# Both norms of a prelude as one factor, router and residual moved beside the feed-forward, value tiles copied by ScalarE

## The chip, the cores and the metric

The kernel runs on one NeuronCore of a Trainium2 chip, as one program in one launch. The metric is the device time of a run in microseconds. In the profile the engines are called PE (TensorE), DVE (VectorE), ACT (ScalarE), POOL (GpSimd) and SP (SyncE, which issues the transfers); PEld is TensorE's weight load.

## What is computed

Four layers, each a cross-attention followed by a feed-forward, on x of 4 x 256 tokens by 256 features (1024 tokens in eight tiles of 128) in float32. Ahead of every block stands a LayerNorm without weights, and x grows by the block's result. The change touches what stands ahead of the feed-forwards of layers 0 and 2. Their input x below is the LayerNorm's output, xn in the kernel:

```python
# layer 0
routed = sigmoid(x @ w_router + b_router) > 0.5
v = rmsnorm(x, norm1_w) @ wv + bv
h = x + v @ wo
h2 = rmsnorm(h, norm2_w)
mlp = (silu(h2 @ w_gate) * (h2 @ w_up)) @ w_down      # 704 wide
out = where(routed, h + mlp, x)

# layer 2: an attention of the tokens among themselves, then experts
h = rms(x, w_ln1)
q, k, v = h @ wq + bq, h @ wk + bk, h @ wv + bv       # 16 heads of 16
q, k = rope(q), rope(k)
scores = where(causal, q @ k.T * 16 ** -0.5, min)
x = x + softmax(scores) @ v @ wo
h = rms(x, w_ln2)                                     # router, 8 experts, a shared one
```

## The kernel before

The program is written by hand, one function for each engine and stage (`dve_pre0` is what VectorE does ahead of the feed-forward of layer 0). Each engine runs its own list in order and waits on semaphores; nothing is scheduled for it. The stages follow each other: latent attention 0, `pre0`, feed-forward 0, folded attention 1, `pre1`, feed-forward 1, folded attention 2, `pre2`, feed-forward 2, latent attention 3, `pre3`, feed-forward 3.

**Norms.** VectorE collects statistics of each tile of x as it is finished (line 245) and aggregates them (L257). The power -1/2 is taken by GpSimd on 8 columns (one for each token tile): `pool_ln` (L273) for the LayerNorm's factor rstd, `pool_pow` (L1747) for the RMS norm's rms_r. VectorE makes xn from x, mean and rstd (L268, eight tiles of 128x256), takes the RMS value out of the variance in three small steps (`dve_norm_ms`, L1759 to L1761), waits for the second power and writes z = xn * rms_r (L1769 in layer 0, L2231 in layer 2).

**pre0.** TensorE folds wv and wo into one matrix and turns bv into a bias row, runs filler matmuls (`pe_warm`, L287, that write to a free bank and are read by nobody), transposes z (L280), and for each tile multiplies by the fold (L1722) and adds the bias by a matmul with the identity (L1724). VectorE scores the router from xn (L1772), adds xn to x (L1776), and then, for each tile, adds the product to xn (L1782), adds it to x where the token is routed (L1785), and sums the squares (L1787). GpSimd takes the power, VectorE writes z2, TensorE transposes it, ScalarE and VectorE split it into a high and a low half-precision part (L1625, L1632), and the feed-forward begins with its first up matmul (L1401).

**Feed-forward.** `dve_ffn` and its sisters run over steps `st`, one for each half of a 128-wide column of hidden features: gate and up products (L1401 to L1403), activation (L1513), products (L1556, L1560), and, `LAG` = 8 steps later, the high part (ACT L1526), the low part (DVE `low`, L1575) and the down product (L1446 to L1448). Feed-forward 0 has 11 steps, so the loop goes on to step 17, and from step 11 on there is only the tail of downs. At its end x takes the sum of each tile out of PSUM (L1594).

**pre2.** GpSimd clears four areas for the value tiles (L2104) after its powers. TensorE transposes z, ScalarE scales it into xT (L2207), and for each of eight tiles TensorE computes q, k (L1961) and v (L1963). VectorE adds the bias to v (L1992) and to q and k (L1993), applies the rotation (L2010, L2012, L2017) and splits the transposed q and k (L1999, L2002); ScalarE makes the high parts (L1979, L1981); GpSimd copies v by head into the cleared areas (L2110). The self-attention runs over 32 steps of four heads' scores (L2032), with the causal mask added by a matmul at each step's end (L2035).

Of the kernel before, what the change touches and what calls it, by code (L numbers as in the profile page):

```python
# [91 lines left out]
def build(nc, d, out):  # L92
    ctx = ExitStack()
    with ctx:
# [98 lines left out]
        def bank(n, k=1):  # L193
# [1373 lines left out]
        def dve_ffn(n, begun=0):  # L1567
# [10 lines left out]
            for st in range(f.steps + LAG - 1):  # L1578
# [11 lines left out]
                if st >= LAG - 1:  # L1590
                    low(st - LAG + 1)
            for i in range(NT):
                dve.wait_ge(s.y_ps, NT // 2 * n + i // 2 + 1)
                dve.scalar_tensor_tensor(x[:, i, :], PS[:, 4 + i // 2, (i % 2) * D:(i % 2 + 1) * D],  # L1594
                                         UNDOWN if n else p0_route[:, i:i + 1], x[:, i, :], ALU.mult, ALU.add).then_inc(ffn_x, 1)
# [99 lines left out]
        p0_score, p0_route, p0_ssq = ffn_v[:, 528:536], ffn_v[:, 536:544], ffn_v[:, 544:552]  # L1695
        p0_junk = ffn_v[:, 1024:1280]
        z = shape3(ffn_s, NT, D)
# [6 lines left out]
        def pe_pre0():  # L1704
# [44 lines left out]
        def pool_pre0():  # L1749
            x_ready(nc.gpsimd, 1)  # L1750
            pool_ln(1)
            pool_pow(pre[0].ms, 1, rms_r[:], rms_e[:], pre[0].r)
# [3 lines left out]
        def dve_norm_ms(me, ready, r_done):  # L1756

            dve = nc.vector
            me.link(dve, dve.tensor_tensor(rms_e[:], rstd[:], rstd[:], ALU.mult))  # L1759
            me.link(dve, dve.tensor_tensor(rms_e[:], rms_e[:], meanvar[:, :, 1], ALU.mult))  # L1760
            dve.tensor_scalar(rms_e[:], rms_e[:], RMS_EPS, None, ALU.add).then_inc(ready, 1)  # L1761
            dve.wait_ge(r_done, 1)

        def dve_pre0():
            dve, s, me = nc.vector, pre[0], own["dve"]
            dve_ln(1)
            dve_norm_ms(me, s.ms, s.r)
            for i in range(NT):
                dve.tensor_scalar(z[:, i, :], xn[:, i, :], rms_r[:, i:i + 1], None, ALU.mult).then_inc(s.z, 1)  # L1769
            dve.wait_ge(s.w, 32)  # L1770
            for i in range(NT):
# [731 lines left out]
```

## Time and profile before

| | us |
|---|---|
| median of three runs | 1309.33 (1308.08 to 1310.52) |
| the profiled execution, its own time | 1310.3 |
| its span (first to last instruction) | 1308.5 |
| PE busy | 1217.0 (93%) |
| DVE busy | 878.1 (67%) |
| ACT busy | 505.6 (39%) |
| POOL busy | 372.8 (28%) |

Times in rows are microseconds from the start of the span. The granted clock of TensorE is a share of its full 2.4 GHz, and 0.979 is its mean over the span. Busy shares are means over all stages.

### The profile page before, as it was taken

How to read it: one execution, taken by the hardware profiler on the slowest of the kernel's cores; microseconds unless marked ns; L12 is line 12 of the kernel's file. 1: busy time of each engine (PE TensorE's matmuls, PEld its weight loads, DVE VectorE, ACT ScalarE, POOL GpSimd, SP SyncE). 2: the span in 40 equal slices, each digit the busy share in tenths (PEclk: the TensorE clock that was granted, in tenths of full speed). 3: DMA queues.
4: the chain of work that ended last, by engine and by line, in shares of the span. 5: the costliest groups of instructions: out<-in, count | busy, mean ns of one | idle time of the engine just before them, and what ended most of it. 6: DMA issues, size and time to landing. Idle time of an engine off the chain costs nothing.

```text
span 1308.5 us, 21984 instructions
## 1 busy us (share of the span) xinstructions
PE 1217.0 (93%) x8541; PEld 790.2 (60%) x8541; DVE 878.1 (67%) x1717; ACT 505.6 (39%) x1133; POOL 372.8 (28%) x385
## 2 busy tenths in 40 slices
PE   6889999999799999999999879998999898999997
PEld 4664658999546565665657545664556565456655
DVE  3776776677376666667667596777766757766666
ACT  3422460111133433433443225652443343555553
POOL 1510115565203333334113320000333333133332
PEclk9899999999899999999999997999999979999999
DMA  4030141000144444444410000000443200233342
GB/s 143 2 153 17 51 141 37 1 1 1 46 174 113 123 124 121 113 113 122 151 58 1 17 1 1 2 2 15 128 122 123 96 17 2 86 115 113 114 133 82
DMA packets 41544, 97.20 MB, mean 74 GB/s; under 512 B 5446, under 2 KB 18246, under 8 KB 39392
## 3 DMA queue, kind: packets, MB, share of 16 engines
q1 hardware_dynamic: 41440, 95.79, 23.8%
q8 instruction: 68, 1.11, 0.4%
q14 instruction: 36, 0.29, 0.1%
HBM read 94.35 MB, written 1.42 MB: 73 GB/s over the span
## 4 chain that ended last, share of the span: by engine, by line
PE 78%; DVE 13%; ACT 3%; issue 3%; POOL 2%; DMA 1%; SPq 0%; DVEq 0%; POOLq 0%; ACTq 0%
PE PS L1401 10%; PE PS L1402 10%; PE PS L1403 10%; PE PS L1446 5%; PE PS L1448 4%; PE PS L1447 4%; PE PS L1036 3%; PE PS L1054 2%; PE PS L1220 2%; PE PS L2050 2%; PE PS L2067 2%; PE PS L1022 2%; PE PS L1024 2%; PE PS L1023 2%; PE PS L2032 1%
## 5 line engine op out<-in xcount | busy, mean ns | idle before, releaser
L1616 POOL TENSOR_TENSOR arena<-arena,m_g 128x512 f32<-128x512 f32 x142 | 183.1, 1291 | 409.9 <-DMA m_g<-gate_rows 240.3
L1401 PE MATMUL PS<-arena 128*128 128x512 f16 x608 | 230.8, 380 | 4.7 <-DVE arena L1632 1.8
L1402 PE MATMUL PS<-arena 128*128 128x512 f16 x608 | 230.8, 380 | 0.0
L1403 PE MATMUL PS<-arena 128*128 128x512 f16 x608 | 230.7, 379 | 0.0
L1446 PE MATMUL PS<-arena 128*128 128x256 f16 x608 | 165.9, 273 | 9.5 <-DVE arena L1573 8.7
L1448 PE MATMUL PS<-arena 128*128 128x256 f16 x608 | 165.7, 273 | 0.0
L1447 PE MATMUL PS<-arena 128*128 128x256 f16 x608 | 165.7, 273 | 0.0
L1513 ACT ACTIVATE arena<-PS 128x512 f32<-128x512 f32 x112 | 66.9, 597 | 245.9 <-PE PS L1403 235.5
L1556 DVE SCALAR_TENSOR_TENSOR arena<-arena,PS 128x512 f32<-128x512 f32 x112 | 77.0, 688 | 124.1 <-ACT arena L1513 123.9
L1573 DVE TENSOR_TENSOR arena<-arena 128x512 f16<-128x512 f32 x142 | 112.0, 789 | 3.9 <-ACT arena L1523 3.9
L1403 PEld LDWEIGHTS PS<-arena 128*128 128x128 f16 x608 | 59.5, 98 | 71.9 <-issue 0.3
L1401 PEld LDWEIGHTS PS<-arena 128*128 128x128 f16 x608 | 59.5, 98 | 65.4 <-DVE arena L1560 2.9
L1523 ACT ACTIVATE arena<-arena 128x512 f16<-128x512 f32 x142 | 88.0, 620 | 22.2 <-PE PS L1448 17.7
L1402 PEld LDWEIGHTS PS<-arena 128*128 128x128 f16 x608 | 59.5, 98 | 58.2 <-issue 0.3
L1102 POOL TENSOR_TENSOR arena<-arena 128x256 f32<-128x256 f32 x96 | 67.6, 726 | 79.3 <-DVE arena L1130 79.3
L1560 DVE TENSOR_TENSOR arena<-arena,PS 128x512 f32<-128x512 f32 x112 | 77.1, 688 | 15.0 <-PE PS L1403 1.0
L1446 PEld LDWEIGHTS PS<-arena 128*128 128x128 f16 x608 | 59.4, 98 | 37.6 <-issue 12.7
L1447 PEld LDWEIGHTS PS<-arena 128*128 128x128 f16 x608 | 59.4, 98 | 19.0
L1448 PEld LDWEIGHTS PS<-arena 128*128 128x128 f16 x608 | 59.4, 98 | 7.0
L2127 ACT ACTIVATE arena<-PS,arena 128x128 f32<-128x128 f32 (+1 forms) x128 | 52.0, 420 | 26.2 <-DVE arena L2141 25.7
L1480 DVE SCALAR_TENSOR_TENSOR arena<-w_stage,arena 128x512 f16<-128x512 f32 x80 | 57.0, 714 | 6.7 <-ACT arena L1475 6.7
L1553 DVE TENSOR_TENSOR arena<-arena,PS 128x512 f32<-128x512 f32 x44 | 30.2, 686 | 45.1 <-PE PS L1403 45.1
(282 smaller groups left out, 2301.2 us busy)
## 6 DMA issues: line engine op xcount, KB each, us to landing
w_stage<-in_up SPq DMA_DIRECT2D x80, 256.0 KB, 2.9
m_g<-gate_rows SPq DMA_DIRECT2D x70, 256.0 KB, 4.2
arena<-in_heads SPq DMA_DIRECT2D x16, 1088.0 KB, 6.5
w_stage<-in_down SPq DMA_DIRECT2D x80, 128.0 KB, 4.1
m_g<-gate_rows SPq DMA_DIRECT2D x17, 512.0 KB, 4.0
m_g<-gate_rows SPq DMA_DIRECT2D x6, 448.0 KB, 4.6
m_g<-gate_rows SPq DMA_DIRECT2D x6, 384.0 KB, 4.1
m_g<-gate_rows SPq DMA_DIRECT2D x6, 320.0 KB, 4.0
```

The source lines that it names most:

```text
L1102: ins = pool.tensor_tensor(r[:, f, :], r[:, f, :], p2[:, 1 - f, :], ALU.add)
L1401: pe.matmul(to, w_hi, x_hi, start=(k == 0), stop=False)
L1402: pe.matmul(to, w_lo, x_hi, start=False, stop=False)
L1403: ins = pe.matmul(to, w_hi, x_lo, start=False, stop=(k == KT - 1))
L1446: pe.matmul(to, h_hi, w_hi, start=(c == 0 and i % 2 == 0), stop=False)
L1447: pe.matmul(to, h_hi, w_lo, start=False, stop=False)
L1448: ins = pe.matmul(to, h_lo, w_hi, start=False, stop=False)
L1523: act.activation(hid_part(0, st % 2), m_c[:, st % 2, :], ACT.Copy).then_inc(s.hi, 1)
L1556: dve.scalar_tensor_tensor(a, t, 1.0, g_ps, ALU.add, ALU.mult).then_inc(s.a, 1)
L1560: dve.tensor_tensor(m_b[:, st % LAG, :], a, u_ps, ALU.mult).then_inc(s.prod, 1)
L1573: dve.tensor_tensor(hid_part(1, st % 2), m_c[:, st % 2, :], hid_part(0, st % 2), ALU.subtract).then_inc(s.lo, 1)
L1616: pool.tensor_tensor(m_c[:, st % 2, :], m_b[:, st % LAG, :], m_g[:, st // 2 % 2, st % 2, :], ALU.mult).then_inc(s.c, 1)
```

## The change

1. **Norms.** `dve_both_norms` takes the place of `dve_ln` and `dve_norm_ms` in `pre0` and `pre2`. The variance of xn is var / (var + 1e-5), so both factors together are (var + 1e-6 (var + 1e-5)) to the power -1/2, and z is written from x directly. GpSimd takes this power first and rstd after it. xn is made later: in `pre0` behind z, in `pre2` one tile at a time inside the self-attention.
2. **pre0.** The bias matmul goes. GpSimd adds the bias row to each xn tile and writes it to p0_h; VectorE adds the product from PSUM to p0_h and sums the squares of the tile before.
3. **Router and residual** of layer 0 go into the feed-forward's loop (`dve_routed`): steps 0 to 7 score a tile each, step 8 makes the masks, steps 8 to 15 write x for a tile each with two instructions.
4. **Filler matmuls**: 30 become 13 ahead of z2 in `pre0`, 41 become 16 ahead of z in `pre2`.
5. **Value tiles.** ScalarE copies v out of PSUM without bias, and GpSimd adds the bias where it copied.
6. **Mask.** In score steps with 128 keys the mask matmuls come first and open the sum; with 256 keys they stay last.

```diff
 # dve_ffn
+                if n == 0:
+                    dve_routed(own["dve"], st)
...
 # pe_pre0
                 for k in range(KT):
-                    pe.matmul(PS[:, 4 + i // 2, (i % 2) * D:(i % 2 + 1) * D], zT[:, k, i, :], p0_fold[:, k, :],
-                              start=(k == 0), stop=False)
-                ins = pe.matmul(PS[:, 4 + i // 2, (i % 2) * D:(i % 2 + 1) * D], ident[:], p0_bias, start=False, stop=True)
+                    ins = pe.matmul(PS[:, 4 + i // 2, (i % 2) * D:(i % 2 + 1) * D], zT[:, k, i, :], p0_fold[:, k, :],
+                                    start=(k == 0), stop=(k == KT - 1))
...
-            pe_warm(30, 3)
+            pe_warm(13, 3)
...
 # pool_pre0
+            pool_pow(s.ms, 1, rms_r[:], rms_e[:], s.r)
             pool_ln(1)
-            pool_pow(pre[0].ms, 1, rms_r[:], rms_e[:], pre[0].r)
+            pool.wait_ge(s.fold, 2)
+            for i in range(NT):
+                pool.wait_ge(ln.xn, NT + i + 1)
+                pool.tensor_tensor(p0_h[:, i, :], xn[:, i, :], p0_bias, ALU.add).then_inc(s.biased, 1)
...
+        def dve_both_norms(me, m, s):
+            dve = nc.vector
+            for i in range(NT):
+                ins = dve.bn_aggr(meanvar[:, i, :], stats[:, i, :])
+            me.link(dve, ins)
+            dve.tensor_scalar(var_e[:], meanvar[:, :, 1], LN_EPS, None, ALU.add).then_inc(ln.var, 1)
+            dve.wait_ge(ln.var, m + 1)
+            dve.scalar_tensor_tensor(rms_e[:], var_e[:], RMS_EPS, meanvar[:, :, 1], ALU.mult, ALU.add).then_inc(s.ms, 1)
+            dve.wait_ge(s.r, 1)
+            for i in range(NT):
+                dve.tensor_scalar(z[:, i, :], x[:, i, :], meanvar[:, i, 0:1], rms_r[:, i:i + 1],
+                                  ALU.subtract, ALU.mult).then_inc(s.z, 1)
...
 # dve_qkv, biased(i)
-                dve.tensor_tensor(sa_v[:, i, :], PS[:, 2 + i % 2, 0:D], p2_bias[:, 2 * D:3 * D], ALU.add)
...
 # act_qkv
+            def copied(i):
+                act.wait_ge(s.qkv, i + 1)
+                act.activation(sa_v[:, i, :], PS[:, 2 + i % 2, 0:D], ACT.Copy).then_inc(s.copied, 1)
...
+            for i in range(NT):
+                copied(i)
+                if i:
+                    high(i - 1)
+            high(NT - 1)
...
 # pool_values
-                pool.wait_ge(s.biased, i + 1)
+                pool.wait_ge(s.copied, i + 1)
...
-                    ins = pool.tensor_copy(sa_vm[b][:, k, :, a, a, :], source[:, :, a, :])
+                    ins = pool.tensor_tensor(sa_vm[b][:, k, :, a, a, :], source[:, :, a, :], bias[:, :, a, :], ALU.add)
...
 # dve_self
+                if t % SA_OF_Q == 1:
+                    dve_normed(5, t // SA_OF_Q)
...
 # pe_pre2
-            pe_warm(41, 2)
+            pe_warm(16, 2)
```

How VectorE's list in `pre0` stands before, from the aggregation to the first turn of the per-tile loop (xn and x are the token tiles, rms_e and rms_r the input and output of the power, arena holds z, masks and constants):

```order
L257 BN_AGGR meanvar<-stats 128x2 x8
L259 TENSOR_SCALAR var_e<-meanvar 128x8
L268 TENSOR_SCALAR xn<-x,meanvar,rstd 128x256 x8
L1759 TENSOR_TENSOR rms_e<-rstd 128x8
L1760 TENSOR_TENSOR rms_e<-rms_e,meanvar 128x8
L1761 TENSOR_SCALAR rms_e<-rms_e 128x8
L1769 TENSOR_SCALAR arena<-xn,rms_r 128x256 x8
L1772 SCALAR_TENSOR_TENSOR arena<-xn,arena 128x256 x8
L1776 TENSOR_TENSOR x<-x,xn 128x2048
L1782 TENSOR_TENSOR xn<-xn,PS 128x256
L1785 SCALAR_TENSOR_TENSOR x<-PS,arena,x 128x256
L1787 SCALAR_TENSOR_TENSOR arena<-xn 128x256
```

And now:

```order
L1769 BN_AGGR meanvar<-stats 128x2 x8
L1771 TENSOR_SCALAR var_e<-meanvar 128x8
L1773 SCALAR_TENSOR_TENSOR rms_e<-var_e,meanvar 128x8
L1776 TENSOR_SCALAR arena<-x,meanvar,rms_r 128x256 x8
L1781 TENSOR_SCALAR xn<-x,meanvar,rstd 128x256 x8
L1790 TENSOR_SCALAR arena<-arena 128x2
L1803 TENSOR_TENSOR arena<-arena,PS 128x256 x2
L1796 SCALAR_TENSOR_TENSOR arena<-arena 128x256
L1803 TENSOR_TENSOR arena<-arena,PS 128x256
```

z (L1776) stands ahead of xn (L1781) and behind one power, the router's products and the long add are gone, and a turn of the loop is L1803 and L1796.

GpSimd's list at the same place, where L1750 and L1747 are the same helper's power and L1760 the bias add:

```order
+L1750 TENSOR_TENSOR rms_r<-rms_e,half_neg 128x8
 L273 TENSOR_TENSOR rstd<-var_e,half_neg 128x8
-L1747 TENSOR_TENSOR rms_r<-rms_e,half_neg 128x8 x2
+L1760 TENSOR_TENSOR arena<-xn,arena 128x256 x8
+L1750 TENSOR_TENSOR rms_r<-rms_e,half_neg 128x8
```

The power for z moved ahead of the one for rstd, and eight adds came in between that and the power for z2.

VectorE's list in steps 10 to 13 of feed-forward 0 now (L1575 is `low`, L1493 a low part of a down weight, L1827 and L1828 write x):

```order
L1575 SCALAR_TENSOR_TENSOR arena<-arena 128x512
L1827 SCALAR_TENSOR_TENSOR x<-xn,arena,x 128x256
L1828 SCALAR_TENSOR_TENSOR x<-arena,x 128x256
L1493 SCALAR_TENSOR_TENSOR arena<-w_stage,arena 128x256
L1575 SCALAR_TENSOR_TENSOR arena<-arena 128x512
L1827 SCALAR_TENSOR_TENSOR x<-xn,arena,x 128x256
L1828 SCALAR_TENSOR_TENSOR x<-arena,x 128x256
L1575 SCALAR_TENSOR_TENSOR arena<-arena 128x512
```

Before, this stretch held the L1575 and L1493 rows alone.

## Rows read from the trace of the kernel before

**Rows 1.** Windows: length, busy (count) of PE, PEld, DVE, ACT, POOL; granted clock, DMA

```profile
77.14:110.88 33.74, 29.14 (x140) 20.76 (x141) 27.48 (x98) 7.01 (x18) 4.92 (x3) 0.95 0.37 149
747.11:785.91 38.80, 30.68 (x118) 16.77 (x119) 35.76 (x74) 9.79 (x26) 9.89 (x16) 1.00 0.05 14
...
86.74:90.15 3.41, 3.41 (x14) 3.03 (x14) 3.20 (x16) 2.71 (x8) 0.00 (x0) 0.50 0.99 409
789.88:803.53 13.65, 13.65 (x76) 6.76 (x70) 6.92 (x10) 6.77 (x34) 0.00 (x0) 0.50 0.00 1
```

**Rows 2.** Timeline, norms of layer 0: start, duration, engine, line, operation, count, [idle before]

```profile
78.60 1.65 POOL L273 TENSOR_TENSOR rstd<-var_e,half_neg 128x8 f32<-128x8 f32 x1 [6.94 <-DVE var_e L259]
...
79.86 2.97 PE L287 MATMUL PS<-causal_b,ident_b 128*128 128x512 bf16 x13
...
80.28 2.67 DVE L268 TENSOR_SCALAR xn<-x,meanvar,rstd 128x256 f32<-128x256 f32 x8 [1.83 <-POOL rstd L273]
...
85.19 2.19 DVE L1769 TENSOR_SCALAR arena<-xn,rms_r 128x256 f32<-128x256 f32 x8 [1.75 <-POOL rms_r L1747]
...
85.60 2.97 PE L280 MATMUL PS<-ident,arena 128*128 128x128 f32 x16 [2.77 <-DVE arena L1769]
```

**Rows 3.** Timeline, the per-tile loop of layer 0 and what follows

```profile
95.74 0.42 DVE L1787 SCALAR_TENSOR_TENSOR arena<-xn 128x256 f32<-128x256 f32 x1
...
96.20 0.42 DVE L1782 TENSOR_TENSOR xn<-xn,PS 128x256 f32<-128x256 f32 x1
...
98.32 1.03 PE L1722 MATMUL PS<-arena 128*128 128x256 f32 x4
...
99.18 0.59 PE L1724 MATMUL PS<-arena,ident 128*128 128x256 f32 x2
...
99.61 6.64 PE L287 MATMUL PS<-causal_b,ident_b 128*128 128x512 bf16 x30
...
103.35 0.17 DVE L1789 TENSOR_SCALAR rms_e<-arena 128x8 f32<-128x8 f32 x1
...
110.88 0.39 PE L1401 MATMUL PS<-arena 128*128 128x512 f16 x1 [1.80 <-DVE arena L1632]
```

**Rows 4.** Single lines over the whole span: duration ns min/median/max, first and last start

```profile
L2104 POOL MEMSET arena<- x4: 951/977/978, 739.9 to 743.0; 128x1024 f32 x4
...
L2231 DVE TENSOR_SCALAR arena<-xn,rms_r x8: 334/674/1114, 740.0 to 744.8; 128x256 f32<-128x256 f32 x8
...
L1102 POOL TENSOR_TENSOR arena<-arena x96: 716/726/736, 202.9 to 332.6; 128x256 f32<-128x256 f32 x96
```

**Rows 5.** Timeline, norms of layer 2, one engine at a time

```profile
731.34 9.01 PE L287 MATMUL PS<-causal_b,ident_b 128*128 128x512 bf16 x41
...
733.45 1.64 POOL L273 TENSOR_TENSOR rstd<-var_e,half_neg 128x8 f32<-128x8 f32 x1 [7.12 <-DVE var_e L259]
...
740.03 5.16 DVE L2231 TENSOR_SCALAR arena<-xn,rms_r 128x256 f32<-128x256 f32 x8 [1.75 <-POOL rms_r L1747]
...
747.11 1.95 PE L1961 MATMUL PS<-arena,xT 128*128 128x512 f32 x4 [1.44 <-ACT xT L2207]
```

**Rows 6.** Timeline in feed-forward 1, GpSimd and VectorE

```profile
500.94 1.27 POOL L1616 TENSOR_TENSOR arena<-arena,m_g 128x512 f32<-128x512 f32 x1 [4.24 <-DMA m_g<-gate_rows]
...
501.81 0.95 DVE L1480 SCALAR_TENSOR_TENSOR arena<-w_stage,arena 128x512 f16<-128x512 f32 x1
```

**Rows 7.** Timeline, one tile of the QKV stretch of layer 2, VectorE

```profile
757.58 0.41 DVE L1992 TENSOR_TENSOR arena<-PS,arena 128x256 f32<-128x256 f32 x1
757.91 0.68 DVE L1993 TENSOR_TENSOR arena<-PS,arena 128x512 f32<-128x512 f32 x1
...
761.93 0.41 DVE L1992 TENSOR_TENSOR arena<-PS,arena 128x256 f32<-128x256 f32 x1
```

**Rows 8.** Timeline, the end of feed-forward 0, VectorE

```profile
151.85 0.69 DVE L1575 SCALAR_TENSOR_TENSOR arena<-arena 128x512 f16<-128x512 f32 x1 [0.74 <-ACT arena L1526]
...
153.42 0.69 DVE L1575 SCALAR_TENSOR_TENSOR arena<-arena 128x512 f16<-128x512 f32 x1 [0.55 <-ACT arena L1526]
```

More of the change, by code:

```diff
@@ L1770, in dve_pre0 @@
             dve.wait_ge(s.w, 32)
-            for i in range(NT):
-                me.link(dve, dve.scalar_tensor_tensor(p0_junk, xn[:, i, :], 1.0, p0_router, ALU.mult, ALU.mult,
-                                                      accum_out=p0_score[:, i:i + 1]))
-            me.link(dve, dve.tensor_scalar(p0_route, p0_score, p0_b, 0.0, ALU.add, ALU.is_gt))
             me.link(dve, dve.tensor_scalar(p0_n2s, p0_n2, SPLIT, None, ALU.mult))
-            me.link(dve, dve.tensor_tensor(x[:], x[:], xn[:], ALU.add))
@@ L1971, in pe_qkv @@
             pe.wait_ge(s.biased, NT)
+            pe.wait_ge(s.copied, NT)
             pe.wait_ge(s.qT, NT)
@@ L1975, in act_qkv, with high @@
             act, s = nc.scalar, pre[2]
-            for i in range(NT):
+            def copied(i):
+                act.wait_ge(s.qkv, i + 1)
+                act.activation(sa_v[:, i, :], PS[:, 2 + i % 2, 0:D], ACT.Copy).then_inc(s.copied, 1)
+            def high(i):
                 b, q = divmod(i, QT)
@@ L2027, in pe_scores, with mask @@
             both = [PS[:, n, 0:2 * keys].rearrange("p (a c) -> p a c", a=2) for n in range(8)[score_banks(t)]]
+            def mask(begins):
+                for e in range(2):
+                    ins = pe.matmul(both[e][:, :, keys - P:keys], ident_b[:], mask_self.rearrange("p (a c) -> p a c", a=2),
+                                    start=begins, stop=not begins)
+                return ins
+            if q == 0:
+                mask(True)
             for q_part, k_part in ((0, 0), (0, 1), (1, 0)):
@@ L2031, in pe_scores @@
                     rows = slice(32 * (j % 4), 32 * (j % 4) + 32)
-                    pe.matmul(both[e], sa_qT[rows, b, q, q_part, j // 4, :], sa_kT[rows, b, k_part, j // 4, :, 0:keys],
-                              start=(q_part == 0 and k_part == 0), stop=False)
-            for e in range(2):
-                ins = pe.matmul(both[e][:, :, keys - P:keys], ident_b[:], mask_self.rearrange("p (a c) -> p a c", a=2),
-                                start=False, stop=True)
-            ins.then_inc(s.s, 1)
+                    ins = pe.matmul(both[e], sa_qT[rows, b, q, q_part, j // 4, :], sa_kT[rows, b, k_part, j // 4, :, 0:keys],
+                                    start=(q == 1 and q_part == 0 and k_part == 0), stop=(q == 0 and q_part == 1))
+            (ins if q == 0 else mask(False)).then_inc(s.s, 1)
         def pe_self():
@@ L2227, in dve_pre2 @@
             dve, s, me = nc.vector, pre[2], own["dve"]
-            dve_ln(5)
-            dve_norm_ms(me, s.ms, s.r)
-            for i in range(NT):
-                dve.tensor_scalar(z[:, i, :], xn[:, i, :], rms_r[:, i:i + 1], None, ALU.mult).then_inc(s.z, 1)
+            dve_both_norms(me, 5, s)
             dve.wait_ge(s.w, 48)
```

65 lines of the change are left out of this document (41 added, 24 removed).

## The prediction

> **What bounds the kernel now.** I read the busy shares by stretch first, then the timeline of the two preludes that the diff touches, with the row's releaser for who ends each wait. The kernel is one long chain of stages with no slack between them, so microseconds saved in a stage are saved at the end, provided that they lie on that stage's own chain. What lies there differs by stage. In the prelude of the first feed-forward (77.14 to 110.88 us) nothing runs through: VectorE waits for GpSimd's power, 1.65 us a time, TensorE waits for VectorE's normalised tiles, and after that VectorE's own queue sets the pace [rows 1, 3]. TensorE needs 1.29 us for a tile of the folded product and is done at 99.8, but VectorE's per-tile loop ends at 103.35 [rows 3]. In the QKV stretch of layer 2 VectorE is busy 35.76 of 38.80 us, TensorE 30.68 [rows 1]: VectorE is the bound there. Elsewhere TensorE is, busy for 93% of the span, except in the last steps of a feed-forward, where a value goes round from ScalarE to VectorE to TensorE [rows 8].
>
> **The change, part by part.**
>
> *Norm of layer 0.* Before: one power (78.60), eight normalised tiles in 2.67 us (80.28), three small steps of about 0.2 us, a second power, eight tiles z from 85.19 [rows 2]. After: one small step more, one power (78.8 to 80.45), then z straight from x, eight at 0.33 us. TensorE cannot take them before 82.83, when its 13 filler matmuls end [rows 2]. That is 2.8 us earlier than the 85.60 of before. The second power, now for rstd, runs on GpSimd behind the first while VectorE writes z. Here is the first unknown, the SBUF port. The trace has two cases of it. A tile like z takes 0.334 us alone, and 1.114 us when one of GpSimd's four memsets (0.977 us) is ahead of it: the tile ends just after the memset, four times in a row [rows 4]. And a two-input VectorE instruction issued at 501.81 under a GpSimd add that ends at 502.21 takes 0.95 us and not 0.69 [rows 6, 8]. So I take it that GpSimd's instruction holds VectorE up to its end, for the power too, which no row shows: z then ends at 84.5 instead of 83.1.
>
> *Adds on GpSimd beside VectorE's tiles.* xn now comes behind z, and each xn tile feeds a GpSimd add 128x256 of 0.73 us [rows 4]. Two xn tiles get through before the first add, the other six wait for one add each, at 0.73 + 0.09 us (the memset and tile pair take 1.03 for a memset of 0.95 to 0.98) [rows 4]. xn therefore ends near 90.1, not at 87.2, and a small step on VectorE waits for one more add: the loop starts at 91.0.
>
> *The per-tile loop.* VectorE drops one instruction of three, and the router's eight products and the 2048-column add ahead of it. What is left is one PSUM add (0.34, as 757.58 to 757.91) and one square (0.46, 95.74 to 96.20) [rows 3, 7]: 0.80 a tile, 8 x 0.80 + 0.46 = 6.9, and 0.3 for the first square behind the last GpSimd add: 98.1. TensorE gives its last tile at 84.95 + 8 x 0.86 = 91.8 (0.86 is 98.32 to 99.18, the bias matmul being gone) [rows 3], earlier, so it isn't the bound. 98.1 against 103.35 is 5.3 us gained, and 7.53 us from there to the first up matmul stay [rows 3]. Without any port hold TensorE would set the pace: loop end 93.9, gain 9.4.
>
> *Filler matmuls.* 13 instead of 30 end at 91.8 + 13 x 0.22 = 94.7 [rows 3], z2 comes at 100.3: 5.6 us without work on TensorE. Before, 2.8 us without work (82.83 to 85.60) were followed by 3.41 us at a granted 0.50, which is 1.2 GHz [rows 1, 2]. I expect that again, partly in the 16 transposes of z2 and perhaps in the first up matmuls: 1.5 us lost, 0 to 3.
>
> *Router and residual in the feed-forward.* Steps 0 to 7 get one product (0.46), steps 8 to 15 two (0.92). While ups run, VectorE's gaps and TensorE's extra down work take them. From step 11 on there are only downs; VectorE's idle time there is 0.74 and 0.55 us a step [rows 8], mean 0.65, against 0.92 added, in five steps: 5 x 0.27 = 1.3 us lost. Bounds: 0, if TensorE's matmuls are the slower link, and 3.
>
> Layer 0 together: -5.3 + 1.5 + 1.3 = -2.5 us.
>
> *Norm of layer 2.* The power starts at 733.65 and ends at 735.3; z began at 740.03 [rows 5]. The rstd power now stands ahead of the four memsets. With everything held, z0 waits for the power, z1 to z4 for a memset each: last z at 735.3 + 1.65 + 4 x 1.03 + 3 x 0.26 + 0.3 = 742.2, where it was 745.2. The QKV product starts 3.0 us earlier than 747.11. If the power holds nothing, six z tiles are through before the first memset, the last ends at 739.1, and the gain is 6.1. Filler 16 instead of 41 ends at 731.34 + 16 x 0.22 = 734.9 [rows 5], so TensorE has little to do until 742; a stretch at half clock costs me 0.8 (0 to 2.6), since QKV waits for VectorE anyway.
>
> *Value tiles.* VectorE loses 757.58 to 757.91, 0.33 us in each of eight tiles of 4.35 us [rows 7]: -2.7 us. ScalarE is busy 9.79 us in the stretch, so its copy has room, and TensorE's work (30.68 less 21 filler matmuls of 0.22, over eight tiles: 3.25 us) stays below the 4.02 that VectorE then needs. GpSimd now adds two inputs instead of copying. It is released by ScalarE, about when VectorE's last two-input instruction of the tile runs, and its adds then lie beside PSUM instructions. Cost 0; if they fall on two-input instructions, up to the whole 2.7.
>
> *Mask ahead, xn in the self-attention.* The same eight matmuls per step behind the same wait: 0. Eight xn tiles (0.33 each) go into VectorE's gaps: 0.3, at most 2.6. The spell at half clock from 789.88, 13.65 us [rows 1], follows a wait that stays, so I leave it.
>
> Layer 2 together: -3.0 + 0.8 - 2.7 + 0.3 = -4.6. Sum -7.1 us: 1310.3 of the profiled execution become 1303.2; the median of the three runs, 1309.3, is 1.0 lower, so 1302.
>
> **The port by the skill.** The Trainium skill, "SBUF — State Buffer", section "Who interferes with whom", says that the port pair of VectorE and GpSimd is an exclusive lock, taken for a whole instruction by whoever issues first. By that rule the rstd power holds z as the memset did, which is the forecast; were the lock shorter than the instruction, the first rival below would come out.
>
> **The rivals.**
> - *The power does not hold the port* (its operands are 8 columns), adds and memsets do. Layer 0 gains 1.4 more, layer 2 3.1 more: 1297.5. For it: 1.64 us for 8 columns can hardly be port traffic. Against: nothing shown.
> - *No hold by the adds either*, clock unharmed: -9.4 + 1.3 - 6.1 - 2.7 + 1 = -16, 1293.5. Against it is the 0.95 us of [rows 6].
> - *Part of the gain is given back*: the adds in QKV hold VectorE's two-input instructions by 0.33 us a tile (+2.7), and half clock reaches 3.4 us into the first ups (+1.7): 1306.4. For it: GpSimd's copy is released just ahead of these instructions today, so a small shift brings the adds there.
> - *Slower*: with the filler before layer 2 cut, TensorE stays at half clock through QKV. A tile would take 2 x 3.25 = 6.5 us instead of 4.02, so 8 x 2.5 = 20 us lost against 7.1 gained: 1322. It decides from the third tile on, 7.1 / 2.5 = 2.8. Against it: after idle time the clock came back within 3.41 us when TensorE was busy [rows 1]; for it: the other spell, 13.65 us under busy rows.
> - *The edits gain nothing* because other work sets the stage: excluded in the norms, where VectorE and TensorE both sit idle for the power.
>
> **How the numbers follow.** Forecast 0.45, the power free of the port 0.25, no hold 0.08, part given back 0.17, slower 0.05. About 0.2% (2.6 us) is what a measurement can tell here. Faster by more than that, below 1306.7: the first three and over half of the fourth, 0.87. Same 0.08, slower 0.05. Forecast's own range 1299.5 to 1305; with the neighbours, for eight in ten, 1295.5 to 1306.5.
>
> **What the profile after would show.** z tiles of layer 0: if the first is near 1.7 us long the power holds, if 0.4 it doesn't. xn tiles at about 0.8 us pace beside the adds, or at 0.33. The last square of the loop near 98 us on the span's clock, not 103; QKV tiles 4.0 us apart; the down steps at the end of the first feed-forward 1.7 to 1.8 us apart instead of 1.5. I am wrong if a half-clock stretch lies in QKV, if the z2 power starts later than 99, or if the self-attention stretch grows by over 1 us.

## The result and the profile after

The changed kernel took 1296.11 us (median of 4 runs, 1295.07 to 1297.61). The kernel before took 1309.33 us, the median of three runs; a fourth took 2074.97 us and is left out. These times make a ratio of 0.9899 and 13.2 us. The ratio on record for this set is 0.9874 (95% interval 0.9851 to 0.9897); it does not come out of the times listed with it, and the record does not say why. Two later sets of rounds with the same two kernels gave 0.9899 (0.9877 to 0.9921) and 0.9905 (0.9890 to 0.9920). So the change takes 12 to 13 us off by the times, up to 17 by the first ratio, where 7 were forecast. The profiled execution took 1295.07 us, its span is 1293.2.

I cut both traces at the same instructions (first fold product, first up of each feed-forward, first x of its end, first aggregation of layer 2's statistics, first QKV product, first score, the squares' sum behind the self-attention):

| stretch | before, us | after, us | change | forecast |
|---|---|---|---|---|
| prelude of layer 0, to the first up | 33.72 | 26.57 | -7.15 | -3.8 |
| feed-forward 0, to its first x | 44.23 | 46.16 | +1.93 | +1.3 |
| norm of layer 2, to the first QKV product | 14.65 | 9.21 | -5.45 | -3.0 |
| QKV product, to the first score | 38.79 | 37.10 | -1.70 | -1.9 |
| self-attention | 103.80 | 98.75 | -5.05 | +0.3 |
| all other stretches | 1073.33 | 1075.37 | +2.04 | 0 |

The forecast -1.9 is -2.7 for the value tiles and +0.8 for half clock. The norms and the self-attention are where it missed. One warning on the cuts: with the mask ahead, the first two mask matmuls (0.31 us) lie before the first score, so they count in the QKV stretch and not in the self-attention. Where kernels with the mask first and last are compared below, I cut at the first matmul of the self-attention, mask or score. No run makes the norms' edit, or the prelude's, alone: what each part is worth within the -7.15 and the -5.45 us is read from the timelines.

The timeline of layer 0 after, which answers [rows 2, 3]:

```profile
78.48 1.65 POOL L1750 TENSOR_TENSOR rms_r<-rms_e,half_neg 128x8 f32<-128x8 f32 x1 [7.95 <-DVE rms_e L1773]
80.11 1.81 POOL L273 TENSOR_TENSOR rstd<-var_e,half_neg 128x8 f32<-128x8 f32 x1
80.17 2.67 DVE L1776 TENSOR_SCALAR arena<-x,meanvar,rms_r 128x256 f32<-128x256 f32 x8 [1.83 <-POOL rms_r L1750]
...
82.77 5.98 DVE L1781 TENSOR_SCALAR xn<-x,meanvar,rstd 128x256 f32<-128x256 f32 x8
83.31 6.70 POOL L1760 TENSOR_TENSOR arena<-xn,arena 128x256 f32<-128x256 f32 x8 [1.39 <-DVE xn L1781]
...
86.33 7.07 PE L1726 MATMUL PS<-arena 128*128 128x256 f32 x32
89.38 0.75 DVE L1803 TENSOR_TENSOR arena<-arena,PS 128x256 f32<-128x256 f32 x2
...
95.78 0.17 DVE L1809 TENSOR_SCALAR rms_e<-arena 128x8 f32<-128x8 f32 x1
...
98.11 3.46 PE L280 MATMUL PS<-ident,arena 128*128 128x128 f32 x16 [1.91 <-DVE arena L1812]
...
103.42 0.39 PE L1401 MATMUL PS<-arena 128*128 128x512 f16 x1 [0.55 <-DVE arena L1634]
```

The reader is to see one pair first: z (L1776) runs from 80.17 under the rstd power of 80.11 and keeps 2.67 us for eight tiles, 0.33 each; six of the eight begin before that power ends at 81.92. The power does not hold VectorE. xn (L1781), the same operation, runs under the adds and takes 5.98. In layer 2, which answers [rows 5], z starts with the same power above it and then meets the memsets:

```profile
729.65 1.82 POOL L273 TENSOR_TENSOR rstd<-var_e,half_neg 128x8 f32<-128x8 f32 x1
729.72 4.82 DVE L1776 TENSOR_SCALAR arena<-x,meanvar,rms_r 128x256 f32<-128x256 f32 x8 [1.82 <-POOL rms_r L1750]
...
731.23 4.21 POOL L2157 MEMSET arena<- 128x1024 f32 x4
...
736.06 1.36 PE L1996 MATMUL PS<-arena,xT 128*128 128x512 f32 x2 [1.02 <-ACT xT L2263]
```

The windows after (length, busy of PE, PEld, DVE, ACT, POOL, granted clock, DMA share, GB/s), which answer [rows 1]; the last four are at half clock:

```profile
77.00:103.42 26.42, 23.96 (x107) 17.56 (x108) 22.33 (x69) 7.25 (x18) 11.78 (x11) 0.85 0.47 189
736.06:773.15 37.09, 32.45 (x119) 17.68 (x119) 32.06 (x66) 12.85 (x34) 7.47 (x16) 0.95 0.05 15
...
74.57:81.40 6.83, 6.32 (x15) 4.52 (x16) 3.23 (x17) 0.00 (x0) 2.92 (x2) 0.50 0.51 186
98.47:101.88 3.41, 3.41 (x17) 3.05 (x17) 3.38 (x11) 2.78 (x7) 0.00 (x0) 0.50 0.00 0
736.76:740.17 3.41, 3.41 (x6) 1.69 (x5) 1.00 (x2) 0.19 (x1) 0.00 (x0) 0.50 0.47 154
777.72:781.13 3.41, 3.41 (x23) 2.02 (x22) 2.00 (x4) 2.27 (x13) 0.00 (x0) 0.50 0.00 0
```

The first of the four, a spell, as I call such a stretch at half clock, lies over the fold product and was not there in the kernel before. It doesn't explain the gain: the changed kernel's two other profiles (after_again and after_third, below) ran the fold product at full clock, and there the stretch to the first up took 26.73 us, not 26.57.

The spell in the self-attention, 13.65 us in the kernel before [rows 1], is 3.41 us here. Is that the change's doing?

One QKV tile after, VectorE and GpSimd, which answers [rows 7]:

```profile
754.17 0.42 DVE L2045 TENSOR_TENSOR arena<-PS,arena 128x256 f16<-128x256 f32 x1
754.20 0.88 POOL L2163 TENSOR_TENSOR arena<-arena 128x128 f32<-128x128 f32 x2 [2.71 <-ACT arena L2015]
...
755.28 0.68 DVE L2039 TENSOR_TENSOR arena<-PS,arena 128x512 f32<-128x512 f32 x1
...
756.61 0.75 DVE L2058 TENSOR_TENSOR arena<-arena 128x256 f32<-128x256 f32 x2
...
759.12 0.68 DVE L2039 TENSOR_TENSOR arena<-PS,arena 128x512 f32<-128x512 f32 x1
```

From 755.28 to 759.12 a tile takes 3.84 us, against 4.35 [rows 7]. GpSimd's adds lie beside instructions that read PSUM, L2045 first, not beside the two-input L2058.

The end of feed-forward 0 after, which answers [rows 8]:

```profile
141.27 0.69 DVE L1575 SCALAR_TENSOR_TENSOR arena<-arena 128x512 f16<-128x512 f32 x1
141.87 0.48 DVE L1827 SCALAR_TENSOR_TENSOR x<-xn,arena,x 128x256 f32<-128x256 f32 x1
142.39 0.48 DVE L1828 SCALAR_TENSOR_TENSOR x<-arena,x 128x256 f32<-128x256 f32 x1
142.91 0.69 DVE L1575 SCALAR_TENSOR_TENSOR arena<-arena 128x512 f16<-128x512 f32 x1
```

No idle time is left: VectorE sets the pace, 1.64 us here and 1.98 where a weight's low part comes in.

### The profile page after: what moved, and what is told of

Its sections match the earlier page's. It is cut to its first block, busy times and chain, and to the rows that moved or that the text cites. A ratio compares the mean times of both kernels' runs of the same rounds, so it can differ in the third digit from the quotient of the medians.

```text
span 1293.2 us, 21914 instructions
## 1 busy us (share of the span) xinstructions
PE 1203.8 (93%) x8483; PEld 783.6 (61%) x8483; DVE 882.1 (68%) x1713; ACT 508.9 (39%) x1141; POOL 376.6 (29%) x393
## 3 DMA queue, kind: packets, MB, share of 16 engines
q1 hardware_dynamic: 41440, 95.79, 24.0%
## 4 chain that ended last, share of the span: by engine, by line
PE 76%; DVE 15%; issue 3%; ACT 3%; POOL 1%; DMA 1%; SPq 0%; DVEq 0%; POOLq 0%; ACTq 0%
PE PS L1401 10%; PE PS L1402 10%; PE PS L1403 10%; PE PS L1446 4%; PE PS L1448 4%; PE PS L1447 4%; PE PS L1036 3%; PE PS L1054 2%; PE PS L1220 2%; PE PS L2103 2%; PE PS L1022 2%; PE PS L1024 2%; PE PS L1023 2%; PE PS L2120 2%; DVE small L547 1%
## 5 line engine op out<-in xcount | busy, mean ns | idle before, releaser
L1480 DVE SCALAR_TENSOR_TENSOR arena<-w_stage,arena 128x512 f16<-128x512 f32 x80 | 62.9, 788 | 5.4 <-ACT arena L1475 5.4
```

## The experiments

Theory A: the gain is the removed power and VectorE's removed work; GpSimd's adds and memsets hold VectorE, powers don't, and the spell in the self-attention has nothing to do with the change. Theory B, the rival: the change itself shortened the spell, by the mask or the value tiles.

### One part alone, and one part undone: the mask and the value tiles

**mask_only** is the kernel before with this part of the diff alone:

```diff
+            if q == 0:
+                mask(True)
             for q_part, k_part in ((0, 0), (0, 1), (1, 0)):
...
+            (ins if q == 0 else mask(False)).then_inc(s.s, 1)
```

> The kernel before with the mask's two matmuls ahead of the scores (for steps of 128 keys) and nothing else of the change. By the prediction (the same eight matmuls behind the same wait) it is worth 0: 1309 us, self-attention stretch 103.8 us. Rival, from the trace after, where the period of four such steps went from 10.01 to 9.90 and 12.45 to 12.23 us: 0.1 us a step, 1.3 to 1.5 us over the stretch, so 1308 us. A second question rides on it: the spell at 1.2 GHz from 789.88 us, 13.65 us long in the kernel before and 3.41 us after. If it hangs on this edit, the spell is short here too and the stretch loses about 5 us (1304 us); if it hangs on what comes before the stretch or on where the window of the clock falls, it stays at 13.65 us.

**values_only** is the kernel before with ScalarE's copy of a value tile and GpSimd's add:

```diff
+                act.activation(sa_v[:, i, :], PS[:, 2 + i % 2, 0:D], ACT.Copy).then_inc(s.copied, 1)
...
-                dve.tensor_tensor(sa_v[:, i, :], PS[:, 2 + i % 2, 0:D], p2_bias[:, 2 * D:3 * D], ALU.add)
...
-                    ins = pool.tensor_copy(sa_vm[b][:, k, :, a, a, :], source[:, :, a, :])
+                    ins = pool.tensor_tensor(sa_vm[b][:, k, :, a, a, :], source[:, :, a, :], bias[:, :, a, :], ALU.add)
```

> The kernel before with the value tiles copied by ScalarE and the bias added by GpSimd, nothing else. By the prediction's sum the QKV product loses 0.33 us in each of eight tiles, 2.7 us: 1306.6 us. By the trace after, where VectorE's two-input instruction of 0.94 us also became 0.75 us since GpSimd no longer runs beside it, it is 0.51 us a tile, 4.1 us: QKV stretch (first product to first score) 38.8 to 34.7 us, 1305 us, provided that no half clock falls into its first tile. The spell at 1.2 GHz in the self-attention: stays at 13.65 us if the mask is its cause.

**mask_last** is the changed kernel with the mask behind the scores again:

> The changed kernel with the mask's matmuls back behind the scores. By the periods of the four-step groups the mask ahead is worth 0.1 us a step (9.90 against 10.01, 12.23 against 12.45), 1.3 to 1.5 us in all: self-attention 100.1 us with a short spell, 104 with a long one, the whole 1297.5 us. By the prediction it is worth 0.

mask_only: 0.9990 of before (0.9975 to 1.0006), which alone tells nothing. values_only: 0.9976 (0.9958 to 0.9995). The stretches say more. In both profiles 10.24 us at half clock lay over the start of the QKV product (from 745.36 and 744.73 us), so they compare with each other: it took 41.73 us in mask_only, 41.41 without the 0.31 us of mask matmuls that lie ahead of the first score there, and 37.95 in values_only. The value edit is worth 3.5 us there, not the 2.7 forecast. mask_last: 0.9908 (0.9893 to 0.9923), self-attention 104.04 us, with a long spell. The changed kernel with a long spell (after_again, below) took 102.72 from its first score and 103.03 from its first mask matmul. So the mask ahead is worth 1.0 us in this pair, and not the 1.3 that the first scores alone would say. Behind the spell the same eight score steps repeat every 22.45 us in mask_last and every 22.13 in after_again. The windows, first mask_last, its self-attention and its spell:

```profile
774.07:878.11 104.04, 100.58 (x902) 61.65 (x903) 77.80 (x128) 57.65 (x264) 0.00 (x0) 0.93 0.01 1
778.60:792.26 13.66, 13.54 (x71) 6.76 (x72) 6.92 (x12) 6.82 (x32) 0.00 (x0) 0.50 0.00 1
```

and the changed kernel again, after_again:

```profile
776.32:879.04 102.72, 98.82 (x901) 62.37 (x901) 77.55 (x129) 57.65 (x264) 0.00 (x0) 0.93 0.01 1
780.57:794.23 13.66, 13.55 (x72) 7.01 (x74) 6.99 (x11) 6.88 (x32) 0.00 (x0) 0.50 0.01 1
```

Where the gain of 0.1 us in a step comes from, TensorE of mask_last in a step of 128 keys (L2096 transposes, L2078 scores on 32 rows, L2081 the mask on 128 rows):

```profile
819.47 1.09 PE L2096 MATMUL PS<-ident,arena 128*128 128x128 f32 x8
820.50 0.50 PE L2078 MATMUL PS<-arena 32*128 32x256 f16 x6
```

and the same place in after_again (L2103 transposes, L2078 the mask):

```profile
821.04 1.09 PE L2103 MATMUL PS<-ident,arena 128*128 128x128 f32 x8
821.97 0.38 PE L2078 MATMUL PS<-causal_b,ident_b 128*128 128x256 bf16 x2
```

Eight transposes occupy 1.03 us when a 32-row matmul follows and 0.93 when a 128-row matmul does. The rows show the two prices and not their reason. "The same eight matmuls" have a price that depends on their order.

Neither edit alone gives the short spell: in mask_only it was 6.83 us, in values_only 17.07. But 6.83 is shorter than 13.65, so one profile each doesn't refute Theory B. What does is the same kernel once more.

### The spell: the same kernel again, and fillers

**after_again** and **after_third** are the changed kernel, unchanged.

> The changed kernel once more, unchanged, on the chip and in the rounds of the next ones. Time 1296 us. Its profile is one more look at the spell at 1.2 GHz at the head of the self-attention: in the profiles so far it is short (3.41 us) where it begins 4.38 us or more behind the first score, and 13.65 us where it begins 4.28 us or less behind it, whatever the edits ahead. If that holds, this profile is of one of the two kinds, and the self-attention takes 98.7 or 102.7 us by it. Rival: the spell's length hangs on the kernel, then it is 3.41 us again whatever the offset.

> The changed kernel, unchanged, in the rounds of the next one. Time 1296 to 1300 us; spell in the self-attention 13.65 us if it begins less than 4.3 us behind the first score, 3.41 us if it begins later.

1299.60 and 1299.79 us, the ratios given at the top. The profile of the first had the long spell, that of the second the short one, so the kernel's code does not decide it, and Theory B is gone. All profiles whose self-attention code is that of the changed kernel, sorted by the time from the first score to the spell's start:

| kernel | to the spell, us | spell, us | self-attention, us |
|---|---|---|---|
| pow_wide | 4.09 | 13.66 | 102.64 |
| bias_te | 4.12 | 13.65 | 102.64 |
| one_residual | 4.13 | 13.65 | 102.65 |
| memset_late | 4.19 | 13.65 | 102.67 |
| after_again | 4.25 | 13.66 | 102.72 |
| early_residual | 4.28 | 13.65 | 102.74 |
| more_filler | 4.38 | 3.42 | 98.74 |
| after_third | 4.45 | 3.42 | 98.75 |
| the changed kernel | 4.57 | 3.41 | 98.75 |
| adds_late | 4.73 | 3.41 | 98.76 |

The self-attention takes 4.0 us more when the spell is long. In all ten profiles it is long where it begins at 4.28 us or earlier and short from 4.38 us on; no run set that time on purpose, so this is an order found in the profiles and not a shown cause. With the mask last it was long at 4.53 too, so the border is not the same for other code.

**sa_filler** puts work where TensorE was idle:

```diff
-            pe_warm(8, 7)
+            pe_warm(11, 7)
...
             for t in range(SA_AHEAD):
                 pe_scores(t)
+            pe_warm(7, 3)
             for t in range(SA_STEPS):
                 turned(t)
```

> The changed kernel with 11 filler matmuls instead of 8 behind the QKV product and 7 more between the second step's scores and the first transposes, where TensorE is idle for 0.8 and 1.6 us. If TensorE's idle time there is what lowers the clock in the self-attention, no spell at 1.2 GHz follows within 20 us of the first score, and the self-attention takes 98 us in every execution, 1 to 4.5 us less than in the changed kernel: 1293 us. Rival: the waits of the first steps (for the maxima and exponentials) lower it anyway; then a spell of 3.4 or 13.7 us stays and the time is 1296 us or, if the fillers hold the transposes back, 1297 us.

0.9858 of before (0.9837 to 0.9879), beside 0.9899 for the changed kernel in the same rounds. Its self-attention, and a window from the QKV product to the end of it:

```profile
776.47:874.06 97.59, 94.50 (x908) 60.33 (x908) 77.23 (x128) 57.70 (x264) 0.00 (x0) 1.00 0.01 1
742.71:871.67 128.96, 121.88 (x1015) 75.65 (x1014) 105.81 (x182) 69.69 (x296) 7.47 (x16) 1.00 0.01 3
```

The granted clock is 1.00 over all of it. (The second window begins where an earlier spell ends, 6.83 us over the first QKV tiles.) all_three, below, has the same fillers and no spell from the QKV product to the end of the self-attention. The transposes after the fillers started 2.83 us behind the first score, exactly as early as without (779.30 against 776.47 here, 776.26 against 773.43 in early_residual), so the fillers cost nothing. So TensorE's idle time at the head of the self-attention brings the spell: filled, it is gone in both profiles, and the time is 1294.81 us beside 1299.60.

### What holds VectorE: memsets, adds, powers

**memset_late**, a wait ahead of the four memsets of layer 2:

```diff
+            pool.wait_ge(s.z, NT)
             for b in range(B):
                 me.link(pool, pool.memset(sa_vm[b], 0.0))
```

> The changed kernel with GpSimd's four memsets in layer 2 behind the eighth z tile, not beside the z tiles. If the memsets hold VectorE (z took 4.82 us for eight tiles there, beside 4.21 us of memsets, against 2.67 us in layer 0), z takes 2.7 us, the QKV product starts 2.1 us earlier against the last wait, and the kernel takes 1294 us. Rival: z is slow for a reason of its own (its operands, the statistics behind it): z stays at 4.8 us and the time at 1296 us. A loss is possible where the memsets now lie beside VectorE's router work: up to 4 us.

The z tiles and the memsets of memset_late:

```profile
728.50 2.67 DVE L1776 TENSOR_SCALAR arena<-x,meanvar,rms_r 128x256 f32<-128x256 f32 x8 [1.81 <-POOL rms_r L1750]
...
731.23 2.97 POOL L2158 MEMSET arena<- 128x1024 f32 x3 [0.98 <-DVE arena L1776]
731.28 0.93 DVE L1645 TENSOR_SCALAR arena<-arena 128x18 f16<-128x18 f32 x1
732.25 0.18 DVE L1646 SCALAR_TENSOR_TENSOR arena<-arena 128x18 f16<-128x18 f32 x1
...
733.42 0.69 DVE L1480 SCALAR_TENSOR_TENSOR arena<-w_stage,arena 128x512 f16<-128x512 f32 x1 [1.00 <-ACT arena L1475]
```

z takes 2.67 us instead of 4.82; the memsets hold. Even the small L1645, 0.18 us in the changed kernel, takes 0.93 under one. They don't hold everything: the SCALAR_TENSOR_TENSOR instructions behind it, L1646 and L1480, begin under the next memsets and take 0.18 and 0.69 us, as they do alone. The QKV product starts 1.8 us earlier (7.38 us behind the first aggregation, not 9.21), and the half-clock spell over its first tiles is gone, so it takes 35.39 us, not 37.10. Yet the median is 1296.10 us, a ratio of 0.9873 that no measurement here tells from the changed kernel's, since the earlier start met the long spell (4.19 in the table): 3.5 us won, 3.9 given back.

**adds_late**, GpSimd's bias adds of layer 0 behind the last xn tile:

```diff
             pool.wait_ge(s.fold, 2)
+            pool.wait_ge(ln.xn, 2 * NT)
             for i in range(NT):
```

> The changed kernel with GpSimd's eight bias adds in layer 0 behind the last xn tile, not beside the xn tiles. If the adds hold VectorE while they run (xn took 5.98 us for eight tiles beside 6.70 us of adds, z 2.67 us beside the power), xn takes 2.7 us here and the adds then run into the loop of PSUM adds and squares: its end moves from 95.31 to between 93 and 96 us on the span's clock, the whole by -2 to +1 us. Rival: xn waits for something else, then it stays at 6 us and the end comes 5 us later.

VectorE and GpSimd of adds_late:

```profile
83.02 2.67 DVE L1782 TENSOR_SCALAR xn<-x,meanvar,rstd 128x256 f32<-128x256 f32 x8
...
85.81 5.95 POOL L1761 TENSOR_TENSOR arena<-xn,arena 128x256 f32<-128x256 f32 x8 [3.64 <-DVE xn L1782]
...
86.56 7.07 PE L1726 MATMUL PS<-arena 128*128 128x256 f32 x32
88.55 0.75 DVE L1804 TENSOR_TENSOR arena<-arena,PS 128x256 f32<-128x256 f32 x2 [2.79 <-PE PS L1726]
...
95.79 0.17 DVE L1810 TENSOR_SCALAR rms_e<-arena 128x8 f32<-128x8 f32 x1
```

xn is through 3.06 us earlier on the span's clock, so the adds do hold it. But VectorE then idles 2.79 us for TensorE's first pair of tiles, and the loop ends at 95.79, where it was 95.78 (0.25 us better at most, since this execution's fold product began 0.26 us later). In this execution the hold was real and worth next to nothing: TensorE's product, whose last tile is done at about 93.6, closed in on it. But this profile has the spell over the fold product too (74.78 to 81.61), and it makes TensorE's product late: that starts 9.45 us behind the first fold product here and 9.48 in the changed kernel's first profile, but 7.25 in after_again, after_third and every other changed kernel whose fold ran at full clock. No profile has late adds and a fold at full clock, so there the hold can be worth up to about 2 us more (my estimate, 9.45 - 7.25). The time, 0.9881 of before (0.9843 to 0.9918), leaves that open.

**bias_te** takes the adds away and gives TensorE its bias matmul back:

```diff
+                ins = pe.matmul(PS[:, 4 + i // 2, (i % 2) * D:(i % 2 + 1) * D], ident[:], p0_bias, start=False, stop=True)
...
-                pool.tensor_tensor(p0_h[:, i, :], xn[:, i, :], p0_bias, ALU.add).then_inc(s.biased, 1)
...
-                dve.tensor_tensor(p0_h[:, i, :], p0_h[:, i, :], PS[:, 4 + i // 2, (i % 2) * D:(i % 2 + 1) * D], ALU.add).then_inc(me.sem, 1)
+                dve.tensor_tensor(p0_h[:, i, :], xn[:, i, :], PS[:, 4 + i // 2, (i % 2) * D:(i % 2 + 1) * D], ALU.add).then_inc(me.sem, 1)
```

> The changed kernel with the bias of the fold added by TensorE again (the matmul with the identity) and no add on GpSimd; the PSUM add reads xn. xn takes 2.7 us, since nothing runs beside it. TensorE's product takes 1.29 us a tile instead of 0.86, so it ends 3.4 us later than 92.4 and sets the loop's end: 96.6 us instead of 95.3, the whole 1.3 us slower than the changed kernel. If GpSimd's hold were the only thing that mattered, the end would be 92 us and the whole 3 us faster.

Ratio 0.9902 (0.9871 to 0.9933). Its stretch to the first up is 27.25 us, against 26.57 and against 26.00 in adds_late. xn took 2.67 us, and VectorE waited for TensorE's bias matmul at each of the four pairs:

```profile
87.86 0.75 DVE L1799 TENSOR_TENSOR arena<-xn,PS 128x256 f32<-128x256 f32 x2 [1.46 <-PE PS L1728]
...
90.45 0.42 DVE L1799 TENSOR_TENSOR arena<-xn,PS 128x256 f32<-128x256 f32 x1 [1.49 <-PE PS L1728]
...
93.04 0.42 DVE L1799 TENSOR_TENSOR arena<-xn,PS 128x256 f32<-128x256 f32 x1 [1.03 <-PE PS L1728]
```

**pow_wide** adds a power on 128x32 elements behind the one for z:

> The changed kernel with one more power on GpSimd, on 128x32 elements, right behind the power for z, so that all eight z tiles of layer 0 run beside it. In the changed kernel z ran at 0.33 us a tile beside a power on 128x8 elements (1.81 us). If a power never holds VectorE, z still takes 2.67 us; if it was the small size, z is held and ends with the power or is slower by a part. The whole is slower by the power's length less what hides it, 2 to 6 us, in both cases.

1302.98 us, one run. The power and the z tiles:

```profile
81.09 5.42 POOL L1757 TENSOR_TENSOR arena<-var_e,half_neg 128x32 f32<-128x32 f32 x1
81.16 2.67 DVE L1779 TENSOR_SCALAR arena<-x,meanvar,rms_r 128x256 f32<-128x256 f32 x8 [1.83 <-POOL rms_r L1750]
```

All eight tiles lie inside one instruction of GpSimd and none is held. The instruction's length is not what decides: a power of 5.42 us holds nothing, an add of 0.73 [rows 4] holds. What does decide stays open, since these powers had 8 or 32 columns and these adds 256: no run has a power on 256 columns or an add on 8.

### Fillers ahead of the norms

**more_filler** has `pe_warm(24, 3)` for 13 and `pe_warm(20, 2)` for 16.

> The changed kernel with 24 filler matmuls instead of 13 ahead of the z2 transposes and 20 instead of 16 ahead of layer 2's norm. If TensorE's idle time ahead of these places (1.91 us before the z2 transposes, then 3.41 us at 1.2 GHz from 98.47; the spell from 736.76 over the first QKV tile, which took 4.45 us and not 2.82) is what lowers the clock, one or both spells go: the z2 transposes take 2 us and not 3.46, the first QKV tile 2.8 us and not 4.45, 1 to 3 us together, 1294 us. Rival: the spells come for other reasons and stay, or the fillers themselves hold the transposes back: 1296 to 1297 us.

Ratio 0.9892 (0.9859 to 0.9924), no gain. The transposes of z2 ran at full clock, 2.28 us instead of 3.46, but the first up came only 0.3 us earlier against the fold (26.25 us, not 26.57): ScalarE and VectorE behind them set the pace. The spell over the first QKV tile stayed (736.83 to 740.24); memset_late, whose transposes no longer wait for held z tiles, lost it.

### The residual in the feed-forward

**early_residual** does two router products in each of steps 0 to 3 and the residual in steps 4 to 11; **one_residual** gives GpSimd two adds a tile and VectorE one product:

```diff
+            for i in range(NT):
+                pool.wait_ge(ffn.prod, FFNS[0].steps0 + i + 1)
+                pool.tensor_tensor(x[:, i, :], x[:, i, :], xn[:, i, :], ALU.add)
+                pool.tensor_tensor(p0_h[:, i, :], p0_h[:, i, :], xn[:, i, :], ALU.subtract).then_inc(s.biased, 1)
...
-                me.link(dve, dve.scalar_tensor_tensor(x[:, i, :], xn[:, i, :], p0_other[:, i:i + 1], x[:, i, :], ALU.mult, ALU.add))
```

> The changed kernel with the router's products two a step in steps 0 to 3 and the two residual products of a tile in steps 4 to 11 instead of 8 to 15. The prediction put 1.3 us on the steps that have only downs, the trace after shows 1.93 us for the feed-forward. If VectorE's two extra instructions are the slow link only where no ups run, the stretch from first up to first x goes from 46.16 to 44.6 us or less (44.23 before the change), the whole 1.5 us faster than the changed kernel. Rival: VectorE has no room beside the ups either: the steps 4 to 7 get longer by as much, 46.2 us.

> The changed kernel with h - xn and x + xn made by GpSimd in steps 0 to 7, so that VectorE has one instruction of 0.52 us a tile instead of two. If VectorE's time is the bound of the last steps, the feed-forward takes 44.6 us or less instead of 46.16; GpSimd's 16 adds of 0.73 us lie beside VectorE's instructions in steps 0 to 7 and may hold each by up to 0.73 us, which TensorE hides if it is the bound there. Rival: the hold is larger than TensorE's cover, then the first steps get longer by 1 to 6 us.

early_residual: 46.26 us for the stretch, the rival. The steps with only downs ran at 1.5 us again, but the first `low` came 23.53 us behind the first up, not 22.07. A step with ups leaves VectorE 0.77 or 0.17 us beside one product of the router in the changed kernel; beside two, in early_residual, 0.37, 0.30 and then nothing:

```profile
109.31 0.69 DVE L1556 SCALAR_TENSOR_TENSOR arena<-arena,PS 128x512 f32<-128x512 f32 x1 [0.37 <-ACT arena L1513]
...
111.90 0.69 DVE L1556 SCALAR_TENSOR_TENSOR arena<-arena,PS 128x512 f32<-128x512 f32 x1 [0.30 <-ACT arena L1513]
...
114.82 0.69 DVE L1556 SCALAR_TENSOR_TENSOR arena<-arena,PS 128x512 f32<-128x512 f32 x1
```

one_residual: 45.17 us, 1.0 better, pace 1.46 to 1.54. The other 0.94 over the kernel before is spent ahead of the first `low` (22.72 us behind the first up, 22.00 before the change) and in the steps just behind it. Moving the work within VectorE's list gained nothing; giving part of it to GpSimd gained 1.0 us.

### All three findings together

**all_three** is the changed kernel with memset_late, one_residual and sa_filler.

> The changed kernel with the memsets behind the z tiles (z 2.7 us instead of 4.8, and the start of the QKV product at full clock: 1.8 + 1.7 us), the residual's sums prepared by GpSimd (1.0 us) and the fillers at the head of the self-attention (1.1 us against the short spell, 5.1 against the long one). If the causes are separate, the profile loses 1.8 + 1.7 + 1.0 + 1.1 to 5.1 = 5.6 to 9.6 us, and the time is 8 us below the changed kernel's, 1290 us. Rival: an earlier start brings the spells to other places, as the memset's edit alone did, and less than 4 us are left.

1288.12 us (1286.30 to 1289.19, 5 runs), beside 1299.79 for the changed kernel in the same rounds: 0.9814 of before (0.9801 to 0.9828), 11.7 us below the changed kernel, where 5.6 to 9.6 were expected. Each edit keeps in company what it was worth alone: 45.16 us in feed-forward 0, 7.38 to the QKV product, and these two windows (self-attention, QKV), both at a granted 1.00:

```profile
769.25:866.81 97.56, 94.28 (x906) 60.36 (x908) 77.18 (x128) 57.57 (x264) 0.00 (x0) 1.00 0.01 1
733.85:769.25 35.40, 31.36 (x121) 17.25 (x123) 32.05 (x66) 12.86 (x34) 9.54 (x19) 1.00 0.05 16
```

Against the changed kernel's stretches in the table that is 1.0 + 1.8 + 1.7 + 1.2 = 5.7 us, and 9.7 where the changed kernel has its long spell. The last 2 us of the medians' 11.7 no stretch here explains.

## Why the prediction was wrong in size

The direction and most of the places were right; the size was 7 us where 12 to 13 came (up to 17 by the first ratio).

- **The step that failed first: "GpSimd's instruction holds VectorE up to its end, for the power too".** It doesn't. I had carried a rule from memset and add over to an instruction that no row showed. z ended at 82.84, not 84.5, and in layer 2 the QKV product came 5.45 us earlier, not 3.0. The first rival, "the power does not hold the port, adds and memsets do", is what happened. The forecast gave it 0.25; its own sum, 1297.5, lies 1.4 us from the measured 1296.1, in part by luck, since it shares the forecast's other terms, and those were off too, as the next points say. The power accounts for 1.6 us in layer 0 (89.38 for 91.0, below) and 2.4 in layer 2 (5.45 for 3.0), about 4 of the 6.35 us by which 7.1 falls short of the 13.45 below.
- **The adds hold VectorE**: right (5.98 us for eight tiles, 0.75 each; two free and six held, as forecast). The loop began at 89.38, not 91.0. Their price was 0.25 us at most in adds_late, where the fold ran at half clock and TensorE's product came late; at full clock it is open. The same spell is why the product began at 86.33, not 84.95, in the changed kernel's profile. It cost nothing there, since VectorE was later still: from the first fold product to the loop's end it is 18.93 us, and 18.94 in after_again, with the fold at full clock.
- **The per-tile loop** at 0.80 us: right (90.51 to 91.31). Its end came at 95.78, not 98.1: 1.6 us by its start, the rest since the first square waited for no add (0.3) and since the forecast's 8 x 0.80 + 0.46 counts one square twice: eight adds and eight squares took 6.40 us.
- **Half clock behind the fillers**: it came where forecast (98.47 to 101.88), behind 1.91 us of idle time and not 5.6, and cost 0.3 to 0.5 us (26.57 against 26.24 in all_three, 26.73 in after_again against 26.25 in more_filler), not 1.5. Over the first QKV tiles it cost 1.7 (37.10 against 35.39), not 0.8. "A half-clock stretch lies in QKV" was one of the prediction's own signs of being wrong, although its sum has a term for one; the sign came true.
- **Steps with only downs**: the mechanism was right, the term small: 1.93 us for 1.3, since L1827 and L1828 take 0.52 us each with their link, not 0.46, and since the cover under the ups was thinner than I took it.
- **Value tiles**: the term of 0.33 us a tile was mis-sized. It was 0.51 in the tile shown, and 3.7 us in the stretch at full clock (38.79 to 35.08 in memset_late, to its first mask matmul). The part that I had priced as a risk of +2.7 came with the other sign: before the change GpSimd's copies lay under the two-input instruction (L2012 then, L2058 now: 0.94 us for two then, 0.75 now), and the adds no longer do.
- **"Mask ahead: the same eight matmuls per step behind the same wait: 0"**: wrong by 1.0 us (mask_last).
- **xn in the self-attention** for 0.3: right. mask_last, which has it and the old mask order, took 104.04 us against 103.80, both with a long spell.
- **"The spell follows a wait that stays, so I leave it"**: the wait stays and so does the spell, but its length is not constant. The profiled execution drew the short form, 4.0 us of the table's -5.05.

Like for like, with the long spell on both sides, the change is worth -7.15 + 1.93 - 5.45 - 1.70 - 1.08 = -13.45 us, 0.9897 of 1308.5. The later ratios, 0.9899 and 0.9905, agree, and so do the times of the first set; that set's own ratio, 0.9874, stays unexplained. The +2.04 us in the other stretches holds no edit: its parts (+1.46, -1.58 and +1.91 in the last feed-forwards and the prelude between them) come and go with the half-clock spells there in every profile.

## What to carry to other kernels

A rule on who holds whom is a rule on one kind of instruction until a row shows another: look for the operation itself, or give both cases equal chances. Before you price a hold, ask what closes in behind it: in adds_late, removing 3 us of it moved the loop's end by 0.25 us at most. And look whether what closed in was itself late by chance, as the half-clock fold was there. Idle time of TensorE can cost twice, once as idle time and once as the half clock that follows (5.1 us in the self-attention, 102.72 against 97.59): compare spells over several profiles of the same kernel before you credit a change with them, then fill the gap.

## What the runs showed of the hardware that I had not expected

- A GpSimd power leaves VectorE's one-input tiles alone for its whole length (1.82 and 5.42 us, z at 0.33 us a tile each time), while adds and memsets of about 1 us hold them. The Trainium skill, "SBUF — State Buffer", section "Who interferes with whom", says of VectorE's 2-port modes, which it says `tensor_scalar` can enter, that whoever issues first has the shared pair for the whole instruction. For add and memset the trace agrees (xn 5.98 us beside the adds and 2.67 without, z 4.82 beside the memsets and 2.67 without); for the power the measurement decides against it.
- Eight transposes take 1.03 us ahead of a matmul on 32 rows and 0.93 us ahead of one on 128 rows.
- Spells at half clock were 3.4, 6.8, 10.2, 13.7 or 17.1 us long, and a difference of 0.1 us in where one began (4.28 against 4.38 us behind the first score) went with a difference of 10 us in its length and 4 us in the time.
